# Turning two of four attention outputs later in their slot, and normalising them behind the scan

## What is computed

```python
x = x + xattn(layernorm(x), ctx_2048)   # 16 heads of 16; queries and output int8 fake-quantised; 1601 keys per batch
x = x + attn(layernorm(x))              # selective scan: dt, B, C projected from x; 16 states per channel
x = x + ffn(layernorm(x))               # mixture of 64 experts, top 8, capacity limited
```

## Time and profile before

| | |
|---|---|
| median of 3 runs | 2306.09 us (2305.89 to 2307.5) |
| the profiled execution | 2303.75 us |
| its span | 2302.0 us |
| PE busy | 2101.8 us, 91% |
| DVE busy | 1752.8 us, 76% |
| ACT busy | 1444.5 us, 63% |
| mixer phase | from 0 to about 1800 us |

### The profile page before, as it was taken

How to read it: one execution, slowest core, us unless ns; L and a number is a source line. 1 busy time by engine, 2 the same in 40 slices (tenths; PEclk the granted TensorE clock), 3 DMA queues, 4 the chain that set the end, 5 groups by cost and what they waited for, 6 DMA issues and landing times. The chain is left out here.

```text
span 2302.0 us, 56038 instructions
## 1 busy us (share of the span) xinstructions
PE 2101.8 (91%) x21448; PEld 1454.3 (63%) x21448; DVE 1752.8 (76%) x3728; ACT 1444.5 (63%) x3012; POOL 677.5 (29%) x646
## 2 busy tenths in 40 slices
PE   7999999999999999999999999999997149999975
PEld 5666666666666666666666666666665037777754
DVE  5557887979797878888888888887978736656646
ACT  2667676868676767676767767676767124445433
POOL 1002040404031322213130404040403437777770
PEclk9999999999999999999999999999999569999998
DMA  7585662323131313232323233232320136676648
GB/s 225 195 283 208 235 256 70 113 81 89 72 88 72 93 67 93 74 86 77 88 84 101 88 72 105 55 105 56 109 51 32 54 119 211 198 232 209 202 137 329
DMA packets 132711, 294.16 MB, mean 128 GB/s; under 512 B 21899, under 2 KB 89143, under 8 KB 126304
## 3 DMA queue, kind: packets, MB, share of 16 engines
q1 hardware_dynamic: 114016, 255.89, 35.2%
q0 software_dynamic: 18432, 34.69, 4.3%
HBM read 165.40 MB, written 108.27 MB: 119 GB/s over the span
## 5 line engine op out<-in xcount | busy, mean ns | idle before, releaser
L799 ACT ACTIVATE sb_probs<-S,sb_negmax 128x1604 f32<-128x1604 f32 x256 | 409.4, 1599 | 246.7 <-DVE sb_negmax L977 246.3
L791 ACT ACTIVATE sb_probsT<-W 128x384 f32<-128x384 f32 (+1 forms) x1024 | 473.9, 513 | 66.3 <-PE W L637 63.6
L637 PE MATMUL W<-sb_ident,sb_probs 128*128 128x128 f32 (+1 forms) x3328 | 484.1, 280 | 23.3 <-DVE sb_o_tok L990 11.9
L977 DVE TENSOR_REDUCE sb_negmax<-S 128x1 f32<-128x1604 f32 x256 | 465.8, 1820 | 2.4 <-PE S L627 1.2
L637 PEld LDWEIGHTS W<-sb_ident,sb_probs 128*128 128x128 f32 (+1 forms) x3328 | 363.0, 139 | 148.4 <-issue 68.5
L610 PE MATMUL W<-sb_wkv_in,sb_ctx 128*128 128x256 f32 (+1 forms) x1664 | 409.0, 388 | 14.9 <-ACT sb_probsT L791 7.2
L600 PE MATMUL W<-sb_ctx,sb_wkv_in 128*32 128x401 f32 x4096 | 399.5, 504 | 4.9 <-DVE sb_V L971 2.5
L610 PEld LDWEIGHTS W<-sb_wkv_in,sb_ctx 128*128 128x128 f32 (+1 forms) x1664 | 292.0, 186 | 76.9 <-ACT sb_probsT L791 26.2
L1330 POOL DMA_INDIRECT y_scratch<-sb_ys,sb_places x256 | 264.0, 1031 | 111.3 <-issue 104.8
L961 DVE SCALAR_TENSOR_TENSOR sb_K_lo<-W,sb_pair_cols,sb_K_hi 128x401 fp32r<-128x401 f32 x256 | 162.0, 633 | 171.5 <-ACT sb_K_hi L783 171.3
L783 ACT ACTIVATE sb_K_hi<-W,sb_pair_cols 128x401 fp32r<-128x401 f32 x256 | 153.2, 598 | 218.2 <-PE W L600 218.2
(11 more groups left out here) (188 smaller groups left out, 2918.7 us busy)
## 6 DMA issues: line engine op xcount, KB each, us to landing
sb_ctx<-ctxT SPq DMA_DIRECT2D x32, 1604.0 KB, 7.6
xe_scratch<-sb_none SPq DMA_DIRECT2D x32, 1088.0 KB, 13.4
sb_xg<-xe_scratch SPq DMA_DIRECT2D x64, 544.0 KB, 4.2
sb_BC<-bc_scratch SPq DMA_DIRECT2D x32, 1024.0 KB, 6.0
sb_Q_hi<-sb_q_hi SPq DMA_DIRECT2D x128, 128.0 KB, 4.5
sb_Q_lo<-sb_q_lo SPq DMA_DIRECT2D x128, 128.0 KB, 5.4
y_scratch<-sb_none SPq DMA_DIRECT2D x16, 1024.0 KB, 11.3
sb_rows<-y_scratch SPq DMA_DIRECT2D x16, 1024.0 KB, 8.6
```

The source lines that it names most:

```text
L637: ins = pe.transpose(W[0:keys_in(t), at * P:(at + 1) * P], probs[n % 2][:, t * P:t * P + keys_in(t)], ident[:])
L791: act.activation(probsT[k][n % (k + 1)][:, 0:wide], ring[bank_of("T", G, k)][:, 0:wide], ACT.Copy)\
L799: act.activation(probs[n % 2][:].rearrange("p (c k) -> p c k", c=QUADS), scores_of, ACT.Exp, bias=negmax[:, slot:slot + 1], accum_out=den[ ...
L977: dve.tensor_reduce(negmax[:, slot:slot + 1], scores_of, AX.XY, ALU.max, negate=True).then_inc(max_done, 1)
```

## The change

`O0` and `O1` move from place 0 to place 1 of their slots: PE turns them behind T3, just ahead of `times_v`, and the ring's order there becomes T0, T1, V, T2, T3, O, K. DVE's `norm_o` of a place 1 output stands behind `scan_unit` (ahead of `sum_unit` where that isn't late) rather than ahead of `v_up`. `O2` and `O3` stay. Waits and banks are computed from the order, so they follow it.

```diff
-       (8, 0): ["XQ"], (8, 1): ["Q"], (10, 0): ["O0"], (14, 0): ["O1"], (1, 0): ["yT"],
+       (8, 0): ["XQ"], (8, 1): ["Q"], (10, 1): ["O0"], (14, 1): ["O1"], (1, 0): ["yT"],
...
                     rest_b(p, m, link)
                     if 0 <= m - FIRST_DECAY - 1 < UNITS:
                         scan_unit(p, m - FIRST_DECAY - 1, link)
-                        if m - FIRST_DECAY - 1 not in SUMMED_LATE:
-                            sum_unit(p, m - FIRST_DECAY - 1, link)
+                for job in small_at(G, 1):
+                    if job[0] == "O":
+                        norm_o(job[1])
+                if mix:
+                    if 0 <= m - FIRST_DECAY - 1 < UNITS and m - FIRST_DECAY - 1 not in SUMMED_LATE:
+                        sum_unit(p, m - FIRST_DECAY - 1, link)
                 if slot == 6 and i >= 2:
```

## The result

| | before | after |
|---|---|---|
| median of 4 runs each | 2306.8 us (2305.89 to 2309.68) | 2322.21 us (2320.59 to 2323.45) |
| the profiled execution | 2303.75 us | 2322.08 us |
| its span | 2302.0 us | 2320.3 us |

The ratio is 1.0066, with a 95% interval of 1.0051 to 1.0081: 0.7% slower.

A forecast was written before the change was run, and what follows sets the result against it. The prediction took PE, DVE and ACT to bound the kernel as one loop, so late K products delay everything. Terms 14.0 + 0.7 + 1.4 = 16.1 us on 2306.1 gave 2322.2 us, range 2315 to 2327.

The forecast's parts named there:

- signs named ahead of the run: Trace: V, T3 waits gone; K waits about 30 times, 14 to 22 us; O waits for V copy; pair 111.0 us.
- The release: Slots 10 and 14: ACT's copy of T2 frees K's bank 0.65 us after the copy starts.
- The alternative of 2326: Copy of T2 priced by the skill page: each of some 30 waits 0.13 us longer, result 2326.
- Slot 10: Middle pair: K starts at 757.82 instead of 757.33, so K_lo reaches DVE 0.49 us later.
- Slot 14: Middle pair: K starts 0.48 us later, K_lo at 786.52 instead of 786.01, 0.51 us later, all of it counting.
- A middle pair: Pairs 1 to 14: 0.49 + 0.51 = 1.00 us more each, 14.0 us in all.
- Pair 0: V products but no scan: 0.2 us in slot 10 and 0.49 in slot 14, sum 0.7.
- The last pair: Slot 10, without V: K's wait ends at 1744.74 instead of 1743.09, K_lo 1.4 us later; slot 14 costs nothing.
- PE's readiness for K: Slot 10: PE ready for K at 757.03, 0.30 us earlier than before; upper bound 757.36.
- The moved `norm_o`: DVE, slots 10 and 14: 0.69 us less ahead of the V copy, 0.69 more behind the scan, nothing in sum.
- K doesn't wait: Rival, 7%: T2's bank is free when PE is ready; slot 10 gains 0.3 us a pair, slot 14 nothing; 2301.9.
- PE is the bound: Rival, 4%: removed idle times come back as gain, 1.06 us in 14 pairs and 0.4 in pair 0; 2291 us.

The follow-up runs named there:

- e12: Kernel before, order untouched, with one wait added: K in slots 10 and 14 waits until ACT has copied T2; 2323.95 us against 2308.46, ratio 1.0073.
- e1: Changed kernel with T2's copy on ACT moved ahead of the exponentials in slots 10 and 14; ratio 0.9984 to the kernel before.
- e4: Changed kernel with `norm_o` right behind `v_up`, ahead of the scan, in slots 10 and 14; ratio 1.0063 to the kernel before.
- e9: Kernel before with the first two additions of scan unit 1's sum moved ahead of K_lo in slot 10; ratio 0.996.
- e11: Changed kernel with `O1` back, slot 10's T2 copy ahead of the exponentials, one unit 1 addition ahead of K_lo; 2298.21 us against 2308.46 before, ratio 0.9958.
- e7: Kernel before with `O0` and `O1` left out, neither turned nor normalised; ratio 0.9933.
- e6: Changed kernel with `O0` behind K in slot 10, `O1` back, unit 1 summed ahead of K_lo, `norm_o` behind it; ratio 0.998 to the kernel before.

## Why the prediction was right, point by point

**The mechanism held.** K's bank passed from `v_up` on DVE to the copy of T2 on ACT, which stands behind the exponentials. e12 gives the cost back with that wait alone, e1 takes it away with that copy alone. Of the signs named ahead of the run, V's and T3's waits went, K's entry came 30 times with 21.0 us in all (forecast 14 to 22), O waits for the V copy, and a pair takes 110.93 us (forecast 111.0).

**The release was sized well.** The copy lets K start 0.64 us after its own start in slot 10 (762.04 to 762.68); forecast 0.65, from T0's 0.55 and one tile more. The alternative of 2326 doesn't bear on this kernel: the budget of the Trainium skill (ScalarE: Activation LUTs, "Rules for kernel authors") is for an ACTIVATE whose bias is a pointer operand, and this copy (L791) is given none. The trace's 0.594 us decides. With that budget falls the reason given for the upper end of the range, 2327.

**Slot 10: 0.43 and not 0.49.** The step that failed is "K_lo follows K_hi by 0.71". K came 4.08 us after the start of the maximum; it had been 3.61, taking that start from the exponentials in the earlier trace rows less the 1.86 us between the two. That is 0.47 later, as forecast. But K_lo came 0.63 after K_hi (764.30 to 764.93); in e4, where it came 0.70 after, slot 10 grew by 0.50. **Slot 14: 0.45 and not 0.51**: from K to K_lo it was 2.28 us before, which I had put at 1.60 + 0.71 = 2.31, and it is 2.25 now.

**A middle pair** was 0.90 and not 1.00; the 14 pairs, maximum to maximum, took 12.4 us more and not 14.0, as single slots of two of them were up to 0.1 shorter. **Pair 0** grew by 0.18 in slot 10 (6.71 to 6.89) and 0.50 in slot 14 (6.39 to 6.89), 0.7 in all, as forecast.

**The last pair: 2.7 and not 1.4.** The end of K's wait was right, again 0.64 behind the copy. The term I had left out is K's own duration: 1.35 us more, at the lower clock. Without it, in e12, the same wait cost 1.44, as forecast.

**The sum** of these terms is 12.4 + 0.7 + 2.8 = 15.9 us (0.1 of it from slot 14 of the last pair), close to the forecast 16.1, because -1.6 and +1.4 cancel. That this, and the median of 2322.21 against 2322.2, agree so well is luck; the two medians differ by 15.4, the two profiled executions by 18.3. Of the latter, 2.4 us lie outside the slots counted: 1.3 from the last maximum to the start of the expert phase, 1.2 later, and -0.2 ahead of the first maximum. I can't assign them.

**PE's readiness for K** was put at 757.03, at the most 757.36, that is 3.31 to 3.64 us after the maximum's start. In e1, where nothing holds K, it started 3.41 after it. The difference of 0.10 is in the transposition of O: the products start 0.26 us after it (761.08 to 761.34) and not 0.15, a figure for which the prediction named no row. It cost nothing in the changed kernel, as K had to wait anyway.

**The moved `norm_o`** was costed at nothing. That held only because K's wait is now there: e1 shows 0.12 us in slot 14 once it isn't. It ended 5.13 us after the maximum's start (763.73), just where forecast.

**The rivals.** "K doesn't wait" (7%) falls with K's entry in the waits. Its price, 0.3 a pair in slot 10 and nothing in slot 14, was too high for its own premise: e1 gained 0.18 in slot 10, lost 0.12 in slot 14, and nothing was left over the 14 pairs. "PE is the bound" (4%) falls with e1 too: the idle times of V and T3 are gone there as well, and the pair is no more than 0.06 us shorter.

## What to carry to other kernels

In a ring of buffers given out in turn, moving one job changes who frees the buffer of every job behind it in the slot. Before you count the waits that go, list for each later job the engine that frees its buffer now, and what stands in that engine's queue ahead of the release. In a loop of three engines the waits of the busiest one (91% here) may bring nothing: look for the idle time on the engine that waits last, and fill it with work that stands behind that wait (e9 to e11, 0.4%). Price the longest wait by itself: here 1 wait of 30 cost 2.7 of 16 us, half of it by slower matmuls behind it.

## What the runs showed of the hardware that I had not expected

- TensorE's granted clock fell in 3 of 4 kernels in which K stood behind a wait of 2.6 to 2.9 us (K then took 2.90, 2.90 and 2.09 us), and in none in which it waited 0.95 us or less (1.51 to 1.55). One profile of each doesn't tell what separates e12 from the other three: its wait, 2.62 us, was the shortest.
- K_lo starts 0.70 to 0.71 us after K_hi where DVE's last instruction ahead of it is the scan's 512-wide product (before, e4, e7, e12), and 0.63 after it where that is the 64x64 multiplication of `norm_o` (after, e1), although DVE has been idle for 0.57 to 1.31 us in between. e4 differs from the changed kernel in the place of `norm_o` alone, so that place makes the difference; why isn't shown.
- In e6 and e7 K_hi comes 2.56 us after K, though the copies ahead of it on ACT are done 0.62 us earlier and K's 16 matmuls take 1.55. It does so in pairs in which POOL issues the indirect DMAs of L522 in that slot, and not in pair 1, which has none there (1.82 us). Whether they are the cause stays open.
